# Turning some score tiles before their exponential in a masked attention over eight batches

## The reference

```python
x = _ln(src) * (1.0 + scale) + shift
q, k, v = ...                                     # B = 8, 16 heads, S = 512, head size 16
scores = einsum('bhqd,bhkd->bhqk', q / sqrt(HEAD_DIM), k) + attention_bias
scores = where(src_mask, -inf, scores)
probs = softmax(scores, axis=-1)
ctx = einsum('bhqk,bhkd->bhqd', probs, v)
x = x + (ctx @ Wo + bo)
return x + _gelu2((_ln(x) * g2 + beta2) @ W1 + b1) @ W2 + b2
```

## Time and profile before

| | |
|---|---|
| median of 3 runs | 1148.03 us (1146.23 to 1148.14) |
| profiled execution | 1158.13 us, its span 1156.3 us |
| granted TensorE clock over the span | 0.963 |
| TensorE busy | 1036.1 us (90%) |
| VectorE busy | 914.4 us (79%) |
| ScalarE busy | 770.2 us (67%) |
| GpSimd busy | 659.4 us (57%) |
| DMA moved | 269.42 MB, mean 233 GB/s |

### The profile page before, as it was taken

How to read it: one execution, slowest core, us unless ns; L and a number is a source line. 1 busy time by engine, 2 the same in 40 slices (tenths; PEclk the granted TensorE clock), 3 DMA queues, 4 the chain that set the end, 5 groups by cost and what they waited for, 6 DMA issues and landing times.

```text
span 1156.3 us, 18947 instructions
## 1 busy us (share of the span) xinstructions
PE 1036.1 (90%) x6843; PEld 766.5 (66%) x6916; DVE 914.4 (79%) x2017; ACT 770.2 (67%) x1253; POOL 659.4 (57%) x327
## 2 busy tenths in 40 slices
PE   5999999996579879979979899899799979999998
PEld 4878889885445545545545455455455569999998
DVE  5599999998789888888878888788888766555543
ACT  6755666574477768868968778688688844444444
POOL 2567666754574686777865866667668432222220
PEclk9999999998799989989989999899899989999999
DMA  8747777596799996988888879879887322111001
GB/s 234 265 143 255 272 257 257 187 379 264 264 342 317 361 328 226 330 298 300 307 297 298 303 244 312 302 283 325 308 297 264 113 93 71 58 55 37 19 20 37
DMA packets 102896, 269.42 MB, mean 233 GB/s; under 512 B 7426, under 2 KB 63490, under 8 KB 86290
## 3 DMA queue, kind: packets, MB, share of 16 engines
q1 hardware_dynamic: 102802, 268.21, 66.3%
HBM read 217.57 MB, written 50.61 MB: 232 GB/s over the span
## 4 chain that ended last, share of the span: by engine, by line
PE 53%; DVE 14%; ACT 12%; issue 9%; DMA 7%; SPq 2%; POOL 2%; DVEq 0%; another core or an unknown queue 0%; ACTq 0%; POOLq 0%
PE psH L535 11%; PE psT L648 11%; PE psV L661 10%; PE psO L535 8%; ACT t_bt L892 6%; PE psS L637 5%; DMA t_mk<-in_mask_Bx1xSxS_bk 4%; ACT t_pt L778 3%; PE psQ L535 3%; DVE t_x L1019 2%; DVE psS L1214 2%; SPq L254 2%; PE psA L535 2%; DVE t_x L1024 1%; PE psX L690 1%
## 5 line engine op out<-in xcount | busy, mean ns | idle before, releaser
L1434 POOL TENSOR_TENSOR t_bt<-t_bt,t_mb 128x1024 f32<-128x1024 f32 x192 | 413.0, 2179 | 175.4 <-DMA t_bt<-in_fside_Bx16xSxS 175.3
L1214 DVE CUSTOM_DVE_ANT_0 psS<-psS,t_bt 128x512 f32<-128x512 f32 x512 | 347.3, 704 | 76.1 <-PE psS L637 60.5
L892 ACT ACTIVATE t_bt<-psS,t_nm 128x512 f32<-128x512 f32 x512 | 338.4, 698 | 60.9 <-DVE t_nm L1214 59.5
L648 PE MATMUL psT<-t_idf,t_bt 128*128 128x128 f32 x2048 | 316.8, 279 | 23.8 <-DVE t_pt L1224 14.6
L648 PEld LDWEIGHTS psT<-t_idf,t_bt 128*128 128x128 f32 x2048 | 259.9, 144 | 81.2 <-DVE t_pt L1224 25.8
L778 ACT ACTIVATE t_pt<-psT 128x512 f32<-128x512 f32 x307 | 185.3, 604 | 89.6 <-PE psT L648 86.8
L637 PE MATMUL psS<-t_ks,t_qs 128*128 128x512 bf16 x455 | 176.8, 389 | 14.3 <-ACT t_bt L892 12.3
L661 PE MATMUL psV<-t_pt,t_vs 128*17 128x512 f32 x1024 | 142.3, 631 | 35.4 <-ACT t_pt L778 29.8
L637 PEld LDWEIGHTS psS<-t_ks,t_qs 128*128 128x128 bf16 x512 | 50.1, 98 | 147.7 <-ACT t_bt L892 109.0
L1224 DVE COPY t_pt<-psT 128x512 f32<-128x512 f32 x205 | 140.5, 685 | 1.8 <-PE psT L648 1.3
L1365 POOL TENSOR_SCALAR t_crs<-t_cmv 128x4 f32<-128x4 f32 x8 | 4.2, 520 | 143.6 <-DVE t_cmv L1011 143.6
(11 more groups left out here) (173 smaller groups left out, 2051.7 us busy)
## 6 DMA issues: line engine op xcount, KB each, us to landing
t_bt<-in_fside_Bx16xSxS SPq DMA_DIRECT2D x128, 1024.0 KB, 5.9
sc_qk<-t_parts SPq DMA_DIRECT2D x32, 768.0 KB, 6.6
t_qs<-sc_qk SPq DMA_DIRECT2D x16, 1024.0 KB, 9.6
t_ks<-sc_qk SPq DMA_DIRECT2D x16, 1024.0 KB, 12.1
t_wo_f<-in_L_cond_Wo SPq DMA_DIRECT2D x8, 1024.0 KB, 7.6
sc_qk<-t_parts SPq DMA_DIRECT2D x16, 512.0 KB, 7.4
t_wi_f<-in_L_cond_Wi SPq DMA_DIRECT2D x7, 1024.0 KB, 5.1
sc_v<-t_v SPq DMA_DIRECT2D x8, 544.0 KB, 7.6
```

The source lines that it names most:

```text
L648: ins = e.transpose(psT[n % NTB][:, kk, :], bt[u % NB][:, t, kk * 128:(kk + 1) * 128], idf[:, :])
L892: e.activation(p, psS[bank(n)][:, :], ACT.Exp, bias=nm[:, n % 16:n % 16 + 1], scale=-1.0).then_inc(a_exp, 1)
L1214: e.tensor_tensor_reduce(s, s, bt[u % NB][:, t, :], -1.0, 3.0e38, ALU.add, ALU.min, nm[:, n % 16:n % 16 + 1]).then_inc(v_max, 1)
L1434: e.tensor_tensor(bt[u % NB][:, hs, :], bt[u % NB][:, hs, :], mb[b % 2][:, hs, :], ALU.add).then_inc(g_M, 1)
```

## The change

Tiles go in pairs, two tiles of one unit. Of five pairs in a row, the pairs 1 and 3 are "turned first": VectorE's pass writes the negated sum over the bias in SBUF in place of PSUM, a second instruction on VectorE subtracts the column of `nm` from it (`shift`), TensorE turns this tile, and ScalarE takes the exponential of the whole pair straight out of PSUM on its way to `pt`. The pairs 0, 2 and 4 have their exponential before they are turned, as all tiles had, and are then evicted by ScalarE as pairs, 128x1024 in one instruction. VectorE evicts no turned tile any more. `psT` is two buffers of two banks each, and `psS` three banks (two before tile 21). The reading of the masks moves from VectorE to ScalarE, `read_any` reads the columns of `nm` of the first head, and the four context steps come one tile later (CLAG = 2). `shifted(n)` counts the turned-first tiles up to n and `exped(n)` the others; the lines with @@ name the engine and the function. The core of the diff:

```diff
-NB, NP, NS, NTB, EARLY, MORE = 5, 6, 4, 3, 5, 21
+NB, NP, EARLY, MORE = 5, 6, 5, 21
-LAG, XLAG, PSTEP, SLAG, FIRST = 4, 1, 2, 12, 20
-ON_ACT = (0, 2, 4)
+LAG, XLAG, PSTEP, CLAG, SLAG, FIRST = 4, 1, 2, 2, 12, 20
+TURNED_FIRST = (1, 3)
 def bank(n):
-    return n % 3 if n < MORE else (n - MORE - 1) % NS
+    return n % 2 if n < MORE else (2, MORE % 2, 1 - MORE % 2)[(n - MORE) % 3]
 def depth(n):
-    return 3 if n < MORE else NS
+    return 2 if n < MORE else 3
...
+def turned_first(n):
+    return n // 2 % 5 in TURNED_FIRST
+def shifted(n):
+    full, rest = divmod(n + 1, 10)
+    return full * 2 * len(TURNED_FIRST) + sum(turned_first(i) for i in range(rest))
+def exped(n):
+    return n + 1 - shifted(n)
...
-            psS = [psum(st, f"psS{i}", [128, 512]) for i in range(3)]
-            psT = [psum(st, f"psT{i}", [128, NT, 128]) for i in range(NTB)]
+            psS = [psum(st, f"psS{i}", [128, 512]) for i in range(2)]
+            psT = [psum(st, f"psT{i}", [128, 2, NT, 128]) for i in range(2)]
             psV = psum(st, "psV", [128, 512])
-            psS.append(psum(st, "psS3", [128, 512]))
+            psS.append(psum(st, "psS2", [128, 512]))
...
             def load_mask(b):
                 if b > 1:
-                    P.wait_ge(v_na, b - 1)
-                    P.wait_ge(v_mb, 4 * (b - 2))
+                    P.wait_ge(a_mb, NT * (b - 1))
...
@@ TensorE, scores(n)
-                P.wait_ge(a_exp, n - depth(n) + 1)
+                before = n - depth(n)
+                if before >= 0:
+                    if turned_first(before):
+                        P.wait_ge(v_max, before + 1)
+                    else:
+                        P.wait_ge(a_exp, exped(before))
...
@@ TensorE, turn_p(n), p = n // 2
-                P.wait_ge(a_exp, n + 1)
-                if n >= NTB:
...
+                if turned_first(n):
+                    P.wait_ge(v_sub, shifted(n))
+                else:
+                    P.wait_ge(a_exp, exped(n))
+                P.wait_ge(a_pair, p - 1)
                 for kk in range(NT):
-                    ins = e.transpose(psT[n % NTB][:, kk, :], bt[...]...)
+                    ins = e.transpose(psT[p % 2][:, n % 2, kk, :], bt[...]...)
...
@@ TensorE, attention(n)
-                    m = n - LAG - 1 - PSTEP * kk
+                    m = n - LAG - CLAG - PSTEP * kk
                     if 0 <= m < N and m % 16 == 15:
                         context(m // 16, kk)
...
@@ ScalarE
-            def evac(n):
+            def pair_out(p):
+                u, t = divmod(2 * p, NT)
+                P.wait_ge(p_T, 2 * p + 2)
...
+                dst = pt[u % NP][:, :, t * 128:(t + 2) * 128].rearrange("p k (t q) -> p t k q", t=2)
+                src = psT[p % 2][:, :, :, :]
+                if turned_first(2 * p):
+                    e.activation(dst, src, ACT.Exp, scale=-1.0).then_inc(a_pair, 1)
+                else:
+                    copy(dst, src, a_pair)
...
-            def read_mask0(t):
+            def read_mask(b, t):
...
+                e.activation(mb[b % 2][:, t, :], mk[b % 2][:, t, :], ACT.Copy, scale=NEG).then_inc(a_mb, 1)
...
@@ ScalarE, attention(n)
-                if 0 <= n - LAG < N and evac_on_act(n - LAG):
-                    evac(n - LAG)
-                if 0 <= n - XLAG < N:
+                if n < N and n // 64 + 1 < B and n % 4 == 1 and 33 <= n % 64 < 49:
+                    read_mask(n // 64 + 1, n % 64 // 4 - 8)
+                if 0 <= n - LAG < N and (n - LAG) % 2:
+                    pair_out((n - LAG) // 2)
+                if 0 <= n - XLAG < N and not turned_first(n - XLAG):
                     exps(n - XLAG)
...
@@ VectorE
             def read_any(b):
-                    P.wait_ge(v_ch, chain(e.tensor_reduce(na[0][:, :], mb[0][:, :, :], AX.X, ALU.max)))
...
-                e.tensor_scalar(na[b % 2][:, :], na[b % 2][:, :], 0.0, None, ALU.is_ge).then_inc(v_na, 1)
+                P.wait_ge(v_max, 64 * b + NT)
+                P.wait_ge(v_nd, b - 1)
+                e.tensor_scalar(na[b % 2][:, :], nm[:, 0:NT], -0.5 * NEG, None, ALU.is_lt).then_inc(v_na, 1)
-            def read_mask(b, t):
...
...
@@ VectorE, scores(n)
-                e.tensor_tensor_reduce(s, s, bt[...], -1.0, 3.0e38, ALU.add, ALU.min, nm[...]).then_inc(v_max, 1)
+                x = bt[u % NB][:, t, :]
+                e.tensor_tensor_reduce(x if turned_first(n) else s, s, x, -1.0, 3.0e38, ALU.add, ALU.min, nm[...]).then_inc(v_max, 1)
-            def evac(n):
...
+            def shift(n):
+                x = bt[n // NT % NB][:, n % NT, :]
+                P.wait_ge(v_max, n + 1)
+                e.tensor_scalar(x, x, nm[:, n % 16:n % 16 + 1], None, ALU.subtract).then_inc(v_sub, 1)
...
@@ VectorE, attention(n)
-                if n < N and n // 64 + 1 < B and n % 4 == 1 and 33 <= n % 64 < 49:
-                    read_mask(n // 64 + 1, n % 64 // 4 - 8)
                 if n < N:
                     scores(n)
-                if 0 <= n - LAG < N and not evac_on_act(n - LAG):
-                    evac(n - LAG)
+                if 0 <= n - 1 < N and turned_first(n - 1):
+                    shift(n - 1)
```

More of the change, by code:

```diff
@@ L142, in program @@
         p_sc, p_T, p_pv, p_ct = (sem(f"p_{n}") for n in ("sc", "T", "pv", "ct"))
-        a_exp, a_ev, a_cv, a_mb, a_cw = (sem(f"a_{n}") for n in ("exp", "ev", "cv", "mb", "cw"))
-        v_max, v_ev, v_C, v_mb, v_na, v_nd, v_vz = (sem(f"v_{n}") for n in ("max", "ev", "C", "mb", "na", "nd", "vz"))
+        a_exp, a_pair, a_cv, a_mb, a_cw = (sem(f"a_{n}") for n in ("exp", "pair", "cv", "mb", "cw"))
+        v_max, v_sub, v_C, v_na, v_nd, v_vz = (sem(f"v_{n}") for n in ("max", "sub", "C", "na", "nd", "vz"))
         g_M, g_n, g_cw = (sem(f"g_{n}") for n in ("M", "n", "cw"))
@@ L154, in program @@
         half = sbuf(base, "half", [128, NT])
+        na = [sbuf(base, f"na{i}", [128, NT]) for i in range(2)]
         with ExitStack() as st:
@@ L208, in program @@
             vs.append(sbuf(st, "vs1", [128, NT, H, VW]))
-            na = [sbuf(st, f"na{i}", [128, NT]) for i in range(2)]
             den = sbuf(st, "den", [128, NT, H])
@@ L455, in attention_loads @@
                     load_x2(0)
[L456 removed]
+                m = n - LAG - CLAG - 2 - 3 * PSTEP - SLAG
                 if 0 <= m < N and m % 64 == 63:
@@ L627, in scores @@
                 s = psS[bank(n)][:, :]
-                P.wait_ge(a_exp, n - depth(n) + 1)
+                before = n - depth(n)
[4 more added lines that the diff above has]
+                        P.wait_ge(a_exp, exped(before))
                 if not on_pool(u):
[L630 to L633, removed]
+                    P.wait_ge(a_mb, NT * (b + 1))
                     P.wait_ge(v_idb, 1)
@@ L741, in tensor_program @@
                 at += 1
-            P.wait_ge(a_exp, N)
+            P.wait_ge(a_exp, exped(N - 1))
+            P.wait_ge(v_max, N)
             turn_c(0)
-            while at <= N + LAG + 3 * PSTEP:
+            while at <= N + LAG + CLAG + 3 * PSTEP - 1:
                 attention(at)
                 at += 1
-            P.wait_ge(a_ev, evacs(N - 1)[0])
-            P.wait_ge(v_ev, evacs(N - 1)[1])
+            P.wait_ge(a_pair, N // 2)
             turn_c(1)
@@ L907, in context_out @@
                 copy(cv[:, :], psV[:, :], a_cv)
-            def read_mask0(t):
-                P.wait_ge(d_m[0], 16)
-                e.activation(mb[0][:, t, :], mk[0][:, t, :], ACT.Copy, scale=NEG).then_inc(a_mb, 1)
+            def read_mask(b, t):
+                P.wait_ge(d_m[b % 2], 16 * (b // 2 + 1))
+                if b > 1:
+                    P.wait_ge(p_sc, 64 * (b - 1))
+                    P.wait_ge(g_M, masks(16 * (b - 1) - 2, 1))
+                e.activation(mb[b % 2][:, t, :], mk[b % 2][:, t, :], ACT.Copy, scale=NEG).then_inc(a_mb, 1)
             def split_w(w, c):
@@ L954, in scalar_program @@
             for t in range(NT):
-                read_mask0(t)
+                read_mask(0, t)
             at = 0
@@ L1212, in scores @@
                     P.wait_ge(g_M, masks(u, t // 2))
-                P.wait_ge(a_exp, n - 15)
-                e.tensor_tensor_reduce(s, s, bt[u % NB][:, t, :], -1.0, 3.0e38, ALU.add, ALU.min, nm[:, n % 16:n % 16 + 1]).then_inc(v_max, 1)
-            def evac(n):
[L1217 to L1224, removed]
+                if n >= 16:
+                    if turned_first(n - 16):
+                        P.wait_ge(v_sub, shifted(n - 16))
+                    else:
+                        P.wait_ge(a_exp, exped(n - 16))
+                    if n % 64 >= 16 and n % 16 < NT:
+                        P.wait_ge(v_na, n // 64 + 1)
+                x = bt[u % NB][:, t, :]
+                e.tensor_tensor_reduce(x if turned_first(n) else s, s, x, -1.0, 3.0e38, ALU.add, ALU.min, nm[:, n % 16:n % 16 + 1]).then_inc(v_max, 1)
+            def shift(n):
+                x = bt[n // NT % NB][:, n % NT, :]
+                P.wait_ge(v_max, n + 1)
```

(9 more changed lines are left out.)

31 lines of the change are left out of this document (8 added, 23 removed).

## The result

The changed kernel takes 1212.8 us (median of 4 runs, 1206.1 to 1222.8) against 1148.1 us: ratio 1.056, 95% interval 1.047 to 1.065. It is slower by 65 us (54 to 75 by that interval); 95 us were forecast, and the range held it. The profiled execution took 1209.7 us, its span 1207.8, 51.5 us more than the span of the kernel before; that one had been profiled in an execution 10 us above its median.

The account below looks back on a forecast made before the run. No engine was full in attention; the new chain through three score banks would set the pace. Terms 10 + 3 + 82 = +95 us on 1148 gave 1243 us, range 1120 to 1290 us.

Parts of the forecast that it names:

- lock: In attention, VectorE's shifts stand until GpSimd's running operation ends: 102 pairs, 0.8 us passed on each, +82 us.
- chain: In attention, scores, turn, paired eviction and exponential close over two tiles in 2.55 us, with three score banks.
- Work per ten tiles: In attention, ScalarE falls from 10.6 to 9.3 us; VectorE swaps four 0.685 us evictions for four 0.49 us shifts.
- Sum without the lock: In attention, +10 us for the new PSUM loop with mask reading moved, +3 us for two early score banks.
- The mask reading: In attention, 5.0 us a batch on VectorE go; on ScalarE about 1.6 us, plus about 1 us of DMA waiting.
- the early tiles: Before tile 21, two score banks instead of three cost between 0 and 10 us, taken as 3.
- The excess per pair: Two shifts' standing beside GpSimd: first 0.66 us, second 0.47, 0.3 where the first ran free; 1.45 us.
- the passing on: After VectorE's slack in attention, 1.1 us of a pair's standing passes on without a context, 0.5 with; 0.8 average.
- Lighter engines win: In attention, the busiest engine sets the pace, -59 us; with 40 us of lock 1129 us; chance 0.22.
- No lock: In attention, shifts run without meeting GpSimd or in its gaps: 1161 us, 1140 to 1175; chance 0.13.
- Lock and clock: In attention, longer stalls idle TensorE and lower its clock: 50 us more, 1293 us; chance 0.13.

Follow-up runs that it names:

- the run with the accumulator form: Changed kernel with the subtraction in a form that also writes out an accumulator: 1161.6 us, ratio 1.013 to the kernel before.
- the one with short GpSimd operations: Changed kernel with GpSimd adding the mask to only four columns of each tile, a probe that skips required work: 1145.0 us, ratio 0.998.
- the order swapped: Changed kernel, plain subtraction kept, with the exponential ahead of the paired operation on ScalarE: 1182.6 us, ratio 1.033.
- its control: Kernel before with GpSimd adding the mask to only four columns of each tile: 1117.0 us, ratio 0.973.
- the swapped run: Changed kernel with the accumulator-writing subtraction and the exponential ahead of the paired operation on ScalarE: 1127.3 us, ratio 0.982.

## Why the prediction was right, and where its sizes were off

The direction and both mechanisms, lock and chain, were right and are shown by runs. That the range held the result says less: 1120 to 1290 us also holds the 1129 us of the first rival and the 1161 us of the second. Of the signs named beforehand, the shifts (0.47 us shortest, 1.04 mean, 2.45 longest), their ends at GpSimd's ends and the step of 2.5 us came; a batch took 84.2 us where 85 to 95 were named, and ScalarE's busy time in the stage fell by 47 us and not 60.

**Work per ten tiles: right.** The paired eviction takes 1.026 us and the paired exponential 1.023 (1.03 taken), the free shift 0.48 (0.49 taken), the pass into SBUF 0.688 (0.704 taken).

**The chain: right in place and length.** 2.52 us against 2.55; the bank costs 24 us in the kernel before (25 by the same working), and breaking the chain by the order on ScalarE gives 34 us.

**Sum without the lock: right, in part by luck.** +10 and +3 us were forecast; the run with the accumulator form is at +13.0 us, the one with short GpSimd operations at -3.6 us, with the cheaper shift. The sum hides two terms of opposite sign. The mask reading was taken as 8 x 2.4 = 19 us less (17 in the expectation of its run) and measures 24 in the kernel before. The rest, banks and pairs, was taken as 8 x 3.6 = 29 us more and 3 for the early tiles, and measures 1161.6 - 1124.0 = 38 us with the accumulator form (its slower shift counted in), of which the order on ScalarE alone gives back 34. Each term was too small by 5 to 6 us, and the errors took each other out. Whether two banks in the early tiles cost the 3 us stays open: the second batch starts within 0.02 us of before, but lock and mask reading act ahead of it too (with the accumulator form it starts at 384.95 us).

**The lock: right in kind, its term too large.** This is the step that failed in size: +82 us stood in the sum. It measures 51 us against the accumulator form (whose shift costs 0.26 us more when free), 55 us with the order swapped, and 68 us against short GpSimd operations, an edit that also relieves three other VectorE operations per batch (12.5 us over the eight batches) and more ahead of attention, as its control shows. The excess per pair was 2 x (1.039 - 0.48) = 1.12 us and not 1.45: 114 us in all, of which 45 to 60% pass on, and the forecast had 55%. So the passing on was about right and the excess was too large: 0.33 of 1.45 us, a quarter of it, was not there. The passing on had a weak spot of its own: of 1.45 us a slack of 1.3 us leaves 0.15, and the prediction let 0.5 us pass without saying why.

Where the quarter went can be counted. The first shift of a pair was to meet GpSimd in 0.62 of the cases and to stand 1.07 us: 65 of 102 were held (0.64), some by only 0.02 us, and stood 0.73 us on average, 0.47 us a pair and not 0.66. The seconds gave 0.65 us a pair and not 0.77. So GpSimd was met as often as forecast, and a meeting cost less. One reason is in the ends: a held shift ends 0.28 to 0.29 us after GpSimd's operation, a free one lasts 0.48, so a shift loses 0.2 us less than the time that the operation still had to run. The rest of the difference was not explained.

No shift of the 204 stood for two operations: the longest, 2.448 us, leaves 1.97 us of standing, less than one operation of 2.22. The mask reading's stand through two, at 501.74 us, was no guide to this instruction. The Trainium skill ("SBUF — State Buffer", Who interferes with whom) says that the shared pair is held for the whole instruction; read as one instruction and no more, it fits all of the shifts. By that reading the prediction had put the lock a quarter lower, about 62 us, which lies inside the 51 to 68 us measured.

**The rivals.** Lighter engines win: wrong for this kernel. With both obstacles away the swapped run reaches 1127.3 us; that this is near the rival's 1129 is chance, as the rival counted 40 us of lock in it and would have 1089 without. Nor does it beat the lighter masks alone (1124.0). No lock: ruled out by the shifts themselves and by the runs that take it away. Lock and clock: not as a term of 50 us. Its evidence, the half clock behind a gap of 1.36 us, was read too short: from 382 to 386 us TensorE was busy only 1.9 of 4 us. But the granted clock over 344 to 900 us is 0.97 in the changed kernel and in the swapped one with the lock, 1.00 and 0.99 in their counterparts with the accumulator form, so a part of the 51 to 55 us may be clock. How much was not separated.

## What to carry to other kernels

A VectorE instruction with input and output in SBUF can be cheap only beside an idle GpSimd (`tensor_scalar` here: 0.48 us free, 1.04 on average): look up in the trace how long such instructions last while GpSimd works, and price it by that, or try a slower form that does not stand (0.74 us fixed was 51 us better here). When buffers are traded between two uses, follow the chain that now closes one buffer earlier: its length divided by the number of buffers is the pace, and the order of two instructions on one engine can be what sets it (34 us faster with three banks, 9 us slower with four). A bundle of edits can hide a good one: the mask reading alone gave 24 us, and the bundle lost 65. Compare what is left of a bundle with its best part, not only with the kernel before.

## What the runs showed of the hardware that was not expected

A shift that is held by GpSimd ends 0.28 to 0.29 us after GpSimd's operation, all 123 times; in the kernel before the mask reading, which is another operation, is held 17 times of 28 and ends 0.55 us after it. The accumulator form of the subtraction takes 0.742 us for 512 elements where the plain one takes 0.482, and never a stall beside GpSimd; the subtraction from PSUM takes 0.747 us, also without one. The read of the accumulator after a pass is 0.08 us when the pass wrote to SBUF and 0.14 us when it wrote to PSUM. GpSimd pays for the lock too, but little: its mask addition takes 2.22 us on average in the changed kernel, 2.18 in the kernel before and 2.15 with the accumulator form.
